# Layer 2's first product pair: from a plain fp32 step to a split step, and a ring of four rounded halves

## The reference

```python
z = einsum('bhd,bkd,hks->bsd', x0, xk, W) + b     # x0: 39 fields; xk: 39 fields, then 64, then 64
z = relu(z)
xk, direct = z[:, :64], z[:, 64:]                 # the last layer: all 128 are direct
```

## Time and profile before

| | us |
|---|---|
| median of 3 runs | 2600.04 |
| the profiled execution | 2598.88 |
| its span, first to last instruction | 2596.9 |
| TensorE busy (matmul) | 2485.9 (96%) |
| VectorE busy | 2130.2 (82%) |
| GpSimd busy | 1870.6 (72%) |
| ScalarE busy | 1611.3 (62%) |
| mean granted TensorE clock | 0.986 |

### The profile page before, as it was taken

One profiled execution on the slowest core, in us unless ns is written; L12 is line 12 of the kernel. 1 busy time (PEld: TensorE's weight loads), 2 busy tenths in 40 slices (PEclk: granted clock), 3 DMA queues, 4 the chain that ended last, 5 costly groups with the idle time before them and its releaser, 6 DMA issues.

```text
span 2596.9 us, 32395 instructions
## 1 busy us (share of the span) xinstructions
PE 2485.9 (96%) x8718; PEld 1598.2 (62%) x8718; DVE 2130.2 (82%) x1806; ACT 1611.3 (62%) x2055; POOL 1870.6 (72%) x1270
## 2 busy tenths in 40 slices
PE   0899999999999999999999999999999999999989
PEld 0466666666656666666666666666666666666655
DVE  1588888888888888888888888888888888888880
ACT  1566666666666666666666666666666666666653
POOL 6677777787777777777777777777777777765450
PEclk7999999999999999999999999999999999999999
DMA  2767567666756756765676677567667657755730
GB/s 69 152 136 164 128 130 163 143 132 141 165 113 139 166 126 130 160 149 124 143 164 130 130 159 147 124 146 161 126 132 162 144 126 147 161 128 128 160 80 1
DMA packets 214673, 352.47 MB, mean 136 GB/s; under 512 B 34373, under 2 KB 47546, under 8 KB 214546
## 3 DMA queue, kind: packets, MB, share of 16 engines
q1 hardware_dynamic: 194675, 346.95, 61.2%
q0 software_dynamic: 19968, 5.15, 2.3%
HBM read 346.86 MB, written 5.12 MB: 136 GB/s over the span
## 4 chain that ended last, share of the span: by engine, by line
POOL 35%; PE 32%; issue 23%; DVE 4%; ACT 4%; DMA 1%; POOLq 0%; ACTq 0%; SPq 0%; DVEq 0%
POOL Pl L366 16%; POOL emb L360 15%; PE ps L773 9%; PE ps L753 7%; PE ps L763 6%; PE ps L783 5%; POOL dir L390 3%; ACT Ph L494 2%; PE ps L748 2%; DVE ps L666 1%; DVE Pl L671 1%; DMA xb<-x_dram 1%; PE ps L891 1%; DVE P L666 1%; PE ps L883 1%
## 5 line engine op out<-in xcount | busy, mean ns | idle before, releaser
L366 POOL TENSOR_TENSOR Pl<-P,Ph 128x1024 fp32r<-128x1024 f32 x448 | 1070.3, 2392 | 488.5 <-ACT Ph L494 487.1
L666 DVE TENSOR_TENSOR P<-xb,ps 128x1024 f32<-128x1024 f32 x768 | 927.3, 1214 | 66.9 <-DMA xb<-x_dram 61.1
L773 PE MATMUL ps<-Ph,wh 128*128 128x512 f32 x1920 | 901.6, 475 | 16.9 <-ACT Ph L494 11.8
L671 DVE TENSOR_TENSOR Pl<-ps,Ph 128x1024 fp32r<-128x1024 f32 x512 | 627.0, 1225 | 243.2 <-ACT Ph L494 233.9
L494 ACT ACTIVATE Ph<-ps 128x1024 fp32r<-128x1024 f32 x512 | 522.6, 1021 | 381.7 <-DVE ps L666 380.4
L360 POOL DMA_INDIRECT emb<-tbl_in,idx x624 | 599.1, 960 | 162.4 <-issue 143.3
L773 PE MATMUL ps<-Ph,wl 128*128 128x512 f32 x1792 | 706.6, 394 | 0.0
L783 PE MATMUL ps<-Pl,wh 128*128 128x512 f32 x1920 | 686.2, 444 | 19.2 <-POOL Pl L366 19.1
L666 DVE TENSOR_TENSOR ps<-xb,ps 128x1024 f32<-128x1024 f32 x512 | 628.2, 1227 | 73.3 <-ACT ps L500 51.6
L494 ACT ACTIVATE Ph<-P 128x1024 fp32r<-128x1024 f32 x448 | 474.7, 1060 | 217.7 <-DVE P L666 203.3
L763 PE MATMUL ps<-P,wp 128*128 128x512 f32 x1280 | 603.3, 593 | 3.5 <-DVE P L666 3.5
(11 more groups left out here) (56 smaller groups left out, 663.9 us busy)
## 6 DMA issues: line engine op xcount, KB each, us to landing
xb<-x_dram SPq DMA_DIRECT2D x1280, 256.0 KB, 7.8
emb<-tbl_in,idx POOLq DMA_INDIRECT x624
x_dram<-rows_sb SPq DMA_DIRECT2D x64, 78.0 KB
xb<-w_in SPq DMA_DIRECT2D x15, 128.0 KB
xb<-wt_in SPq DMA_DIRECT2D x2, 512.0 KB, 8.4
xb<-dense_in SPq DMA_DIRECT2D x1, 768.0 KB, 5.0
wp<-w_in SPq DMA_DIRECT2D x5, 128.0 KB
xb<-w0a_in SPq DMA_DIRECT2D x1, 409.5 KB
```

The lines of the kernel that those rows point to most:

```text
L366: pool.tensor_tensor(Pl[:, h_slot(ref, c, k)], P[:, p_slot(ref, c, k)], Ph[:, h_slot(ref, c, k)], ALU.subtract).then_inc(low_pool, 1)
L666: dve.tensor_tensor(p, xb[:, x], xk.unsqueeze(1).broadcast_to([128, 2, N]), ALU.mult)\
L671: dve.tensor_tensor(Pl[:, h_slot(ref, c, k)], p_ps, Ph[:, h_slot(ref, c, k)], ALU.subtract)\
L773: pe.matmul(z_of(c, k), w[:, q, j, :], Ph[:, h_slot(ref, c, k), j, :], start=k in (L1B, L2) and i + j == 0, stop=False)
```

## The change

Step 10, layer 2's first pair, becomes V instead of P. HRING becomes 4 instead of 5. Every table that counts steps by kind follows from the string: 16 of the 20 steps are now split, four are plain, and 11 instead of 12 products per chunk go through the ring `P`.

```diff
--- before.py
+++ after.py
@@ -29,11 +29,11 @@
 
 PRE = 4
 L1B, L2, STEPS = PAIRS - PRE, PAIRS, 2 * PAIRS
-KIND = "GVPVGPVGVPPGVGVGVPVG"
+KIND = "GVPVGPVGVPVGVGVGVPVG"
 SPL = [k for k in range(STEPS) if KIND[k] != "P"]
 PLAIN = [k for k in range(STEPS) if KIND[k] == "P"]
 NS = len(SPL)
-PRING, HRING = 4, 5
+PRING, HRING = 4, 4
 XSLOTS = PAIRS + PRE
 TRANSPOSE_AT, X2_AT = 0, 3
 SUM_AT = [3, 5, 7, 9, 11, 13, 15]
```

## The result

The changed kernel takes 2606.63 us (median of nine runs, 2601.93 to 2610.39) against 2600.04 of the kernel before (nine runs, 2598.53 to 2603.33). The ratio is 1.0023, 95% interval 1.0015 to 1.0032: between 3.9 and 8.3 us slower. The forecast was 2596.8, with no change that can be told at 0.50 and slower at 0.16; the forecast's own line between the two was 2605.2. The profiled execution of the changed kernel took 2604.07 us, its span is 2602.2.

The account below looks back on a forecast made before the run. PE was taken to set the pace, at 96% busy with few gaps. The terms -21.1 + 14.4 + 3.0 + 0.5 = -3.2 us took the profiled 2598.9 to 2595.7, or 2596.8 as a median; range 2582 to 2607.

Parts of the forecast that it names:

- PE's own gain: Step 10 on PE takes 1.38 us split instead of 1.71 plain, 0.33 less in each of 64 chunks: -21.1 us.
- Step 10 in time: At step 10, the rounded half is there 1.3 us before PE wants it, so PE never waits: 0.
- the ring: Four slots for rounded halves cost nothing; PE frees the new step's slot by 1078.8, step 14 needs it at 1081.2: 0.
- The second chunk: Step 14's product 1.12 us later shifts ACT's gapless run; PE loses 1.03 waiting for the square, 14 times: +14.4 us.
- The loads: DVE's nine waits for loads outside the usual one per chunk each cost the full 0.33 us: +3.0, bounds 0 to 15.8.
- the loads set the chunk: Rival: the load burst keeps first, third and fourth chunks from getting shorter, leaving only the stall: 2609.6 us, chance 0.10.
- the sign that the forecast had named for it: Chunks other than the second still at 37.5 us or more would mean loads or DVE bind.
- Start and last chunk: One more weight pair in three big copies at the start, one slot less for the last chunk's MLP: +0.5 us.
- the ring's 0.07: Rival: a rounding waits for PE's fourth split step back, so ACT trails PE: 2600 to 2606 us, chance 0.07.
- DVE as the bound: Rival: DVE's five cycles between product 10 and the next chunk's product 0 set the pace; 2611.2 at 3.80 us, chance 0.08.
- room 0.40: At the next chunk's step 0, the shifted product can still be rounded 0.40 us before ACT wants it: cost 0.
- Full gain: Rival: the second chunk's stall does not come: 2582.4 us, or 2589.6 with half the stall; full or half chance 0.20.

Follow-up runs that it names:

- e5: Kernel before, with PE doing step 10 as six fp32r matmuls on still data, DVE, ACT and POOL unchanged: 2585.90 us, ratio 0.9942.
- e3: Kernel before with only the ring of rounded halves cut from five slots to four: 2599.74 us, ratio 0.9997.
- e1: Changed kernel with ACT's two copies of the gathered rows moved in the second chunk from step 15 to 17: 2594.44 us, ratio to before 0.9974.
- e2: Kernel before with ACT's copies of the gathered rows moved to step 17 in the second chunk: 2601.77 us, ratio 1.0002.
- e6: Changed kernel with PE doing step 10 as two plain matmuls on still data, DVE and ACT as changed: 2615.66 us, ratio to before 1.0055.
- e11: Changed kernel with only the load order changed, pairs 2 and 3 behind pair 9: 2600.14 us, ratio to before 0.9995.
- e8: Changed kernel with ACT's copies of the gathered rows at step 17 and loads of pairs 2 and 3 behind pair 9: 2587.71 us, ratio to before 0.9949.
- e9: Kernel before with only the load order changed, pairs 2 and 3 behind pair 9: 2600.07 us, ratio 0.9999.
- e13: e8 with the second chunk's gathers spread, three instead of five ahead of GpSimd's low half of step 4: 2575.45 us, ratio to before 0.9898.

## Why the prediction was wrong, point by point

**PE's own gain (-21.1).** Right in size per chunk: 0.33 where nothing else bound. e5 shows it alone.

**Step 10 in time, the ring (0).** Right as far as it was tried. There is no wait at step 10, and e3 shows the ring at 0 at the old pace; in the changed kernel the rows leave 2.3 us at step 14.

**The second chunk (+14.4).** Right, mechanism, place and size. Forecast: second chunk 39.06 (38.36 - 0.33 + 1.03); measured 38.98. Forecast PE wait at the sum about 1 us; the row shows 0.75 and a matmul that is 0.06 longer. In 14 chunks, as forecast, +0.6 stands where -0.33 was to be had, 13 us; the one with PE's long wait for POOL differs by -0.06. e1, e2 and e6 show it from three sides. The cycle of 3.66 us, read from the earlier trace rows, held in the chunk shown except for the first, 3.58; in the last tile's third chunk all are 3.58.

**The loads (+3.0).** This is the step that failed. I wrote "the burst's end is tied to its amount, not to PE, so a shorter chunk meets the same landing", and then charged it only for nine waits counted in the kernel before. That count says how often a load was late at the old pace, not how often it will be when each chunk comes 0.33 us earlier. Step 4 alone waited for its load in 13 chunks before and in 30 after. In the profiled execution the first chunks lost 16 x 0.33 - 3.2 = 2.1 us of their gain and the fourth 15 x 0.33 - 1.0 = 4.0, both summed over the trace chunk by chunk; in the last tile a late load of step 4 adds 1.3. That is 7.4 where 3.0 were charged, and e11 gives 7 from the runs. The bound of 0 to 15.8 held the value, and the chosen end of it was wrong. The rival "the loads set the chunk" had the mechanism right for half of the chunks; "for it: the full DMA share" was the row that should have weighed more than "one wait per chunk is followed by a wait for ACT", because that wait for ACT was itself about to move. The fourth chunk at 37.51, where near 37.2 was forecast, is the sign that the forecast had named for it.

**Start and last chunk (+0.5).** The second, smaller miss. In the last tile PE's list is shorter and DVE's cycle already sets the pace; five cycles do not hide behind anything there, and one more costs 1.5 us in the third chunk (36.29 in e8, where no load is late there, against 34.78). I had looked at the steady tiles only.

**The sum.** Chunk by chunk the profiled executions differ by -3.2 (first), +8.6 (second), -5.5 (third), -1.0 (fourth chunks), +2.5 for the last two and the end, together +1.4; and by +3.9 before the first chunk begins. The last can't be put down to the change: the row of transposes with which these sums begin starts between 95.7 and 101.0 us in the thirteen kernels' executions, 96.2 before and 100.2 after, 95.7 in e1 with the same start as the changed kernel. The forecast of -3.2 missed the trace's +1.4 by 4.6 us. The loads make 4.4 of that; the smaller misses, the last tile on one side and second and third chunks on the other, nearly cancel. With +1.4 in the trace against the medians' +6.6 (at least +3.9), 2.5 to 5 us stay open: the changed kernel's other runs were on average 2.8 us above its profiled one, and their traces are not there. More late loads in those runs would do it, since e11 removes 7 us in the median; that is argued, not shown. The chances do not add up either: loads 0.10, three quarters of DVE's 0.08 and half of the ring's 0.07 make 0.195 for slower and leave 0.465 for no change, not 0.16 and 0.50.

**DVE as the bound.** Refuted for the steady tiles: room 0.40 at the next chunk's step 0, cost none; DVE at 86% in e8 is 13 us faster than the kernel before. True in the last tile. The Trainium skill's rule ("Perfetto Trace Analysis", Identifying the Most-Contended Engine), that PE is to be judged by MFU and its weight loads' busy share and DVE by occupancy, would have put DVE first going by the weight loads (MFU was not worked out). e5 disagrees: 0.33 us less per chunk on PE, whose weight loads were at 62%, gave 15 us.

**Full gain.** Refuted for the change as it is; e8 has most of it (-13 us) and e5 alone 15.

## What to carry to other kernels

When a change speeds up the engine that sets the pace, every margin in the row of waits shrinks by the same amount. A count of waits taken at the old pace does not price a burst that is already at full rate. A better estimate, which was not tried here, would take the landing times, subtract the gain, and sum what falls below zero. A change that looks like a loss may be a gain behind two lists that were written for the old one: mending the copies and the load order brought nothing that could be told before, and 12 and 7 us after. And look at the tiles at the ends by themselves, where another engine may have the pace.

## What the runs showed of the hardware

In these traces the granted clock of TensorE falls to its lower level in or behind a long wait of PE. In the kernel before, PE waits 4.75 us for POOL, from 757.4 to 762.2:

```profile
762.17 1.22 PE L783 MATMUL ps<-Pl,wh 128*128 128x512 f32 x2 [4.75 <-POOL Pl L366]
763.19 1.91 PE L753 MATMUL ps<-sq,w 117*128 117x512 f32 x2
764.11 1.42 PE L773 MATMUL ps<-Ph,wh 128*128 128x512 f32 x1
765.32 0.63 PE L773 MATMUL ps<-Ph,wl 128*128 128x512 f32 x1
...
768.07 0.63 PE L783 MATMUL ps<-Pl,wh 128*128 128x512 f32 x2
```

The matmuls of 765 us last 0.63 instead of 0.40 and stand 0.43 apart instead of 0.23; in the trace the clock is at 1.2 instead of 2.4 GHz for 6.8 us from 760.4 on. This chunk takes 43.7 to 46.4 us in all thirteen executions, with 3.4 or 6.8 us at the lower level. Another chunk, which starts between 1606 and 1635 us, takes 39.5 to 40.2 in the eight executions in which the clock stayed up and 41.1 to 43.7 in the five in which it fell (e2, e8, e9, e11, e13). PE's longest wait for POOL there is 1.0 to 1.8 us in the eight, 1.8 in e2 and 2.9 to 4.4 in the other four. In e11 POOL stood 6.0 us ahead of a gather in this chunk, in the changed kernel 4.0. Four of the five kernels with reordered loads are among those whose clock fell; why is not known. At the start the clock is at its lower level for 6.8 to 13.7 us between 79 and 119 us.

So from one trace to another the first of these chunks differs by up to 2.7 us, the second by up to 4.2 and the start by up to 5.3, which is as large as the effect of this change. Whether the executions of one kernel differ for the same reason is not shown, since each kernel has one trace. Where the clock falls, a long wait of PE costs twice, once as the wait and once as slow matmuls behind it.
